# One of four transposed score tiles gets its mask from an identity product on TensorE, with a reordered start and smaller steps between

## The reference

```
inv_mask = 1.0 - attention_mask * padding_mask            # streams 0..3 only
scores = einsum('bhqd,bhkd->bhqk', q, k) / sqrt(DEPTH)
scores = scores + mask * -1e9
attn   = softmax(scores);  out = einsum('bhqk,bhkd->bhqd', attn, v)

amax    = max(abs(x2d), axis=-1)                          # int8 layer
x_scale = maximum(amax, 1e-6) / 127
x_q     = clip(round(x2d / x_scale), -128, 127)
out     = (x_q @ weight_q.T) * x_scale * weight_scale + bias
```

## Time and profile before

| | us |
|---|---|
| median of 3 runs | 1570.03 (1567.35 to 1577.67) |
| profiled execution, its own time | 1575.42 |
| its span | 1573.6 |
| PE busy | 1301.5 (83%), 5544 matmul records |
| DVE busy | 946.3 (60%) |
| ACT busy | 668.4 (42%) |
| POOL busy | 493.7 (31%) |
| granted TensorE clock, mean | 0.902 of full speed |

### The profile page before, as it was taken

One profiled execution on the slowest core, in us unless ns is written; L12 is line 12 of the kernel. 1 busy time (PEld: TensorE's weight loads), 2 busy tenths in 40 slices (PEclk: granted clock), 3 DMA queues, 4 the chain that ended last, 5 costly groups with the idle time before them and its releaser, 6 DMA issues. The chain is left out here.

```text
span 1573.6 us, 17765 instructions
## 1 busy us (share of the span) xinstructions
PE 1301.5 (83%) x5544; PEld 569.5 (36%) x5544; DVE 946.3 (60%) x2143; ACT 668.4 (42%) x1238; POOL 493.7 (31%) x676
## 2 busy tenths in 40 slices
PE   3598877878789898987997997997889856999992
PEld 1131232322324233452352352362332333556661
DVE  3699989989796665455546646647767422223334
ACT  1154545545455555535534534535546431112220
POOL 4260533522122222235335335233310103403331
PEclk9698988989899798998998997998989778999996
DMA  3833332322353532212212222223321119822225
GB/s 115 270 116 95 102 102 66 120 62 81 115 134 122 135 103 73 81 54 54 76 60 54 61 75 54 61 74 95 98 86 41 42 40 336 272 62 84 78 69 161
DMA packets 130508, 156.64 MB, mean 100 GB/s; under 512 B 15339, under 2 KB 105967, under 8 KB 130160
## 3 DMA queue, kind: packets, MB, share of 16 engines
q1 hardware_dynamic: 117872, 134.48, 28.7%
q10 hardware_dynamic: 8704, 12.58, 2.6%
q0 software_dynamic: 3840, 8.43, 1.5%
HBM read 93.92 MB, written 63.05 MB: 100 GB/s over the span
## 5 line engine op out<-in xcount | busy, mean ns | idle before, releaser
L1027 DVE TENSOR_REDUCE Mx<-bank 128x1 f32<-128x512 f32 x512 | 342.0, 686 | 304.0 <-PE bank L813 301.8
L727 ACT ACTIVATE prob<-bank 128x512 f32<-128x512 f32 x512 | 290.4, 594 | 281.0 <-PE bank L829 279.3
L813 PE MATMUL bank<-KS,QS 96*128 96x512 bf16 x768 | 319.6, 416 | 76.5 <-DVE Mx L1027 42.9
L829 PE MATMUL bank<-QS,KS 99*128 99x512 bf16 x768 | 317.2, 415 | 63.0 <-DVE prob L1038 28.4
L727 ACT ACTIVATE prob<-prob 128x512 f32<-128x512 f32 x256 | 160.9, 629 | 183.3 <-DVE prob L1038 181.5
L842 PE MATMUL bank<-prob,V 128*17 128x512 f32 x1536 | 231.3, 678 | 0.7 <-ACT prob L727 0.7
L813 PEld LDWEIGHTS bank<-KS,QS 96*128 96x128 bf16 x768 | 77.1, 100 | 302.1 <-DVE Mx L1027 115.1
L829 PEld LDWEIGHTS bank<-QS,KS 99*128 99x128 bf16 x768 | 76.8, 100 | 282.8 <-ACT prob L727 131.1
L561 POOL TENSOR_TENSOR rstd<-ve,minus_half 128x4 f32<-128x4 f32 x28 | 28.7, 1025 | 291.7 <-DVE ve L976 291.7
L581 POOL TENSOR_SCALAR MR<-neg 16x128 bf16<-16x128 f32 x48 | 13.9, 289 | 320.0 <-ACT neg L701 319.9
L1038 DVE TENSOR_TENSOR prob<-bank,ff_h 128x512 f32<-128x512 f32 x128 | 87.8, 686 | 19.1 <-PE bank L829 18.7
(11 more groups left out here) (153 smaller groups left out, 1761.8 us busy)
## 6 DMA issues: line engine op xcount, KB each, us to landing
stack_scr<-parts SPq DMA_DIRECT2D x48, 384.0 KB, 2.6
QS<-stack_scr SPq DMA_DIRECT2D x48, 384.0 KB, 4.0
KS<-stack_scr SPq DMA_DIRECT2D x48, 384.0 KB, 4.8
stack_scr<-parts SPq DMA_DIRECT2D x48, 256.0 KB, 2.9
w_gu<-in_gate_up ACTq DMA_DIRECT2D x16, 512.0 KB, 5.4
disp<-zero SPq DMA_DIRECT2D x2, 3096.0 KB, 16.1
xr<-disp SPq DMA_DIRECT2D x48, 129.0 KB, 2.1
stack_scr<-parts SPq DMA_DIRECT2D x48, 128.0 KB, 2.8
```

Of the source, the lines that this page charges most:

```text
L727: act.activation(prob[:, U % NP_, j, :], src, ACT.Exp, scale=CAST).then_inc(exp_done, 1)
L813: pe.matmul(bankS[i % NS][:, :], QS[0:STACK, v, qt * P:(qt + 1) * P], KS[0:STACK, v, :], start=True, stop=True).then_inc(s_full, 1)
L829: pe.matmul(bankT[e % NT][:, :], KS[0:ROWS, h, kt * P:(kt + 1) * P], QS[0:ROWS, h, :], start=True, stop=True).then_inc(t_full, 1)
L1027: dve.tensor_reduce(dst, b, AX.X, ALU.max).then_inc(s_read, 1)
```

## The change

Nothing is computed otherwise but for rounding. In words:

- **The product.** `PE_MASKED = 3`: in a masked stream tile j = 3 of each unit gets its mask from PE, by an f32 product of the 128x128 identity with the transposed mask (128x512), `start=True`, ahead of the score product, which now adds to it. DVE's add of that tile is gone (64 of 256), ACT exponentiates from the bank, and PE frees that bank by `exp_done` and no longer by `t_masked`.
- **The start.** The first statistics stand ahead of DVE's constants; the ones in `KS` are written by a DMA; the plain mask of sequence 0 is prepared by DVE; its transposed one by POOL, two `cut`s later than before; ACT's table is loaded by a dummy activation.
- **The int8 steps.** `xscale` is computed by POOL, the clamp is one operation of DVE, the rounding one of ACT; `i8T` is up to a step later.
- **Small steps.** `affine` and `res` go in halves; the epsilon is added by POOL's `root` and not by DVE (28 small operations less on DVE, 28 more on POOL).

```diff
+PE_MASKED = 3
...
-            put(late, s, ("turn", p, 0), ("res", p, 0))
+            put(late, s, ("turn", p, 0), *halves("res", p, 0))
...
-            put(late, s - 1, ("mask", p, 0))
+            put(late, s - 1, ("mask", p, 0), ("fill", p, 0))
             put(late, s if p == 0 else max(s, first - 6), ("mask", p, 1))
+            put(late, 5 if p == 0 else max(s, first - 6), ("fill", p, 1))
...
-                put(late, e + 20, ("amax", p), ("res", p, 4))
-                put(early, e + 21, ("quant", p))
-                put(late, e + 22, ("i8T", p))
-                put(early, e + 23, ("i8turned", p))
+                put(late, e + 20, ("amax", p), *halves("res", p, 4))
+                put(early, e + 21, ("xrec", p))
+                put(late, e + 21, ("quant", p))
+                put(early, e + 22, ("clamp", p), ("round", p))
+                put(early, e + 23, ("i8T", p))
+                put(early, e + 24, ("i8turned", p))
...
@@ SP
+                            sp.wait_ge(consts_pool, 8)
+                            sp.dma_start(KS[STACK:ROWS, :, :].rearrange("r h (c q) -> r (h c) q", q=P),
+                                         ones_b[0:ROWS - STACK, :].unsqueeze(1)
+                                         .broadcast_to([ROWS - STACK, H * S // P, P])).then_inc(ones_in, 16)
...
@@ POOL
                 def root(p, i):
                     pool.wait_ge(ve_ready[p], i + 1)
-                    link(pool.tensor_tensor(rstd[p][:, :], ve[p][:, :], minus_half[:, :], ALU.pow))
-                    link(pool.tensor_tensor(shift[p][:, :], mv[p][:, :, 0], rstd[p][:, :], ALU.mult))
-                    pool.tensor_scalar(shift[p][:, :], shift[p][:, :], -1.0, 0.0, ALU.mult, ALU.add)\
+                    pool.tensor_scalar(shift[p][:, :], mv[p][:, :, 0], -1.0, 0.0, ALU.mult, ALU.add)
+                    link(pool.tensor_scalar(rstd[p][:, :], mv[p][:, :, 1], 1e-6 if i in (1, 2, 3) else 1e-5, 0.0,
+                                            ALU.add, ALU.add))
+                    link(pool.tensor_tensor(rstd[p][:, :], rstd[p][:, :], minus_half[:, :], ALU.pow))
+                    pool.tensor_tensor(shift[p][:, :], shift[p][:, :], rstd[p][:, :], ALU.mult)\
                         .then_inc(rstd_ready[p], 1)
...
-                    link(ins)
-                    link(pool.tensor_scalar(T[p][:, :, :], T[p][:, :, :], -MAGIC, 127.0, ALU.add, ALU.min))
-                    pool.tensor_scalar(xq[p], T[p][:, :, :], -128.0, 0.0, ALU.max, ALU.add)\
-                        .then_inc(xq_ready[p], 1)
+                    ins.then_inc(grid_ready, 1)
+
+                def step_of(p):
+
+                    pool.wait_ge(amax_ready, p + 1)
+                    pool.tensor_scalar(xscale[p][:, :], amax[:, :], 1e-6, 1.0 / 127.0, ALU.max, ALU.mult)\
+                        .then_inc(xscale_ready, 1)
...
@@ ACT
-                        if n < B:
-                            act.wait_ge(t_masked, e + 1)
+                        if n < B and j != PE_MASKED:
+                            act.wait_ge(t_masked, U * (HG - 1) + j + 1)
...
+                    elif kind == "round":
+                        p = at[0]
+                        act.wait_ge(clamped, p + 1)
+                        act.activation(xq[p], T[p][:, :, :], ACT.Identity, bias=minus_magic[:, 0:1])\
+                            .then_inc(xq_ready, 1)
...
@@ PE
                     if e >= NT:
                         b = e - NT
-                        pe.wait_ge(t_masked if b < MASKED else exp_done, b + 1)
+                        if b < MASKED and b % HG != PE_MASKED:
+                            pe.wait_ge(t_masked, b // HG * (HG - 1) + b % HG + 1)
+                        else:
+                            pe.wait_ge(exp_done, b + 1)
                     h = g * HG + j
+                    on_pe = n < B and j == PE_MASKED
+                    if on_pe:
+                        if u < QT:
+                            pe.wait_ge(mask_ready[1], QT * n + u + 1)
+                        pe.matmul(bankT[e % NT][:, :], identf[:, :], mb[n % 2][:, QT + kt, :],
+                                  start=True, stop=False)
                     pe.matmul(bankT[e % NT][:, :], KS[0:ROWS, h, kt * P:(kt + 1) * P], QS[0:ROWS, h, :],
-                              start=True, stop=True).then_inc(t_full, 1)
+                              start=not on_pe, stop=True).then_inc(t_full, 1)
...
@@ DVE
-                    link(ins)
-                    dve.tensor_scalar(ve[p][:, :], mv[p][:, :, 1], 1e-6 if i in (1, 2, 3) else 1e-5, None,
-                                      ALU.add).then_inc(ve_ready[p], 1)
+                    ins.then_inc(ve_ready[p], 1)
...
-                    link(dve.tensor_scalar(xscale[p][:, :], amax[:, :], 1e-6, 1.0 / 127.0, ALU.max, ALU.mult))
...
+                def clamp(p):
+
+                    dve.wait_ge(grid_ready, p + 1)
+                    dve.tensor_scalar(T[p][:, :, :], T[p][:, :, :], MAGIC + 127.0, MAGIC - 128.0, ALU.min, ALU.max)\
+                        .then_inc(clamped, 1)
+
+                def first_mask():
+
+                    dve.wait_ge(pm_in[0], 32)
+                    link(dve.tensor_scalar(pm_row[:, :], pm_row[:, :], -1.0, None, ALU.mult))
+                    dve.wait_ge(mask_in[0][0], 16)
+                    for qt in range(QT):
+                        m = mb[0][:, qt, :]
+                        link(dve.tensor_tensor(m, m, pm_row[:, :], ALU.mult))
+                        ins = dve.tensor_scalar(m, m, 1.0, NEG, ALU.add, ALU.mult)
+                    ins.then_inc(mask_ready[0], 1)
...
-                    if n < B and 0 <= u < UNITS:
+                    if n < B and 0 <= u < UNITS and j != PE_MASKED:
                         masked(n, u, j)
```

125 lines of the change are left out of this document (75 added, 50 removed).

## The result

| | before | after |
|---|---|---|
| median, us | 1570.35 (4 runs) | 1548.98 (1542.46 to 1549.26, 4 runs) |
| profiled span, us | 1573.6 | 1547.5 |
| granted clock, mean | 0.902 | 0.920 |
| first transposed tile, us | 79.7 | 63.3 |
| masked stage (from there to stream 4's first), us | 390.5 | 393.2 |

The ratio is 0.9847, with an interval of 0.9805 to 0.989: 24 us less, and 26 by the spans. The forecast was 48 less. The direction was right and the time lies in the range, but about half of the gain isn't there. The last three rows of the table say where in these two executions: the start gave 16.5 (forecast 17), the int8 stage 12 (forecast 18), and the masks, forecast at -12, cost 3.

The account below looks back on a forecast made before the run. DVE (97% busy) was taken to bound most masked steps, PE's queue units 6 to 8, with gains hanging on the loop through PE. Masks -12, start -17, int8 -18, small steps -1: -48, from 1570.0 to 1522; range 1492 to 1560.

Parts of the forecast that it names:

- the start: From kernel start to the first transposed tile: statistics, first cut and first score come earlier; -17 us, bounds -12 and -21.
- the term of the masks, -12: All 64 masked steps: each gives DVE back 0.60 and costs PE 0.85; sum -12 us, bounds -39 and +54.
- Units 0 to 5, "0.1 to 0.2 longer", +5: Masked streams, 24 steps, nearly all with a projection: PE's loop makes each 0.1 to 0.2 us longer, +5 in all.
- the loop of 6.05: Units 0 to 5 with a projection: hand-summed loop through PE of 6.05 us, formerly 5.2, against a measured step of 5.9.
- Units 9 to 15, "I take 0.5" for 21 steps, -10: Streams 1 to 3: each step gains up to 0.55 us, taken as 0.5, over 21 steps: -10.
- The hand-closed loop of 4.27: Units 9 to 15: hand-summed loop through PE after the change, 4.27 us, where DVE's 4.84 was the longer loop before.
- Stream 0's last ten units, -9: Stream 0, units 6 to 15: -0.5 us a step by DVE and 4 us by a higher clock, together -9.
- Units 6 to 8, +2: DVE waits for PE's queue there: product's 0.85 counts whole in unit 6, perhaps a third saved next; +2 over three streams.
- The int8 term, -18: Int8 steps among the unmasked streams: DVE's 4.11 us waits and PE's idling behind them go; -18, bounds -10 and -24.
- a clamp that stands behind POOL: Int8 steps: DVE's new clamp could wait some 1.2 us behind POOL in four sequences, making the sum -43; nothing was added.
- The small steps: 28 operations of 0.17 us leave DVE, most of them where it isn't the bound: -1.
- The rival at 1552: Masks cost +10, start and int8 steps give 28: -18 in all, 1552 us; chance 0.22.

Follow-up runs that it names:

- the timed pairs: Two pairs differing in the f32 product at tile 3 alone: changed kernel without it 0.9764 against 0.9847 with it; kernel before with it alone 1590.21 us, ratio 1.008.
- the eight operations for six: Kernel before with the residual additions of stages 2 and 4 in halves, step size still on DVE: 1580.48 us, ratio 0.999.

## Why the prediction was wrong

**What failed is the term of the masks, -12; it measured +3 in the two profiled executions, and +13 by the timed pairs.** The prediction wrote off DVE in units 0 to 5 and closed the loop through PE by hand, and it put that loop too short; elsewhere it counted more steps that gain than there are. By its own steps, in the two traces:

- *Units 0 to 5, "0.1 to 0.2 longer", +5.* They were 0.46 to 0.67 longer: +12.6 over four streams. The loop was the right one, and DVE was rightly written off there; it was closed 0.30 short (product 0.96 for 0.85, 0.32 for 0.22, 0.51 for 0.42). Over a measured step of 5.9 the loop of 6.05 left 0.15; with the 0.30 it is 0.45, three times that. The product's price came from half a projection, and it holds where the product follows a score tile without a pause (0.86, 252.74 to 253.60 at tile 1). Right behind the values it is 0.96, and that is where it stands in these steps. At tile 1, where it never stands behind the values, 25 products start 0.22 after the tile ahead of them and keep PE 0.86; 37 start 0.34 or more after it and keep it 0.96.
- *Units 9 to 15, "I take 0.5" for 21 steps, -10.* They gave 6.6 over three streams, of which clock dips in streams 1 and 3 are a part. In stream 2, units 11 to 14 gained 0.45, 0.36, 0.13 and 0.95; units 9, 10 and 15, which hold turnings and a projection, gained nothing or lost up to 0.45. The hand-closed loop of 4.27 is in the trace with 4.37 to 4.39, but I counted seven plain steps where there are four.
- *Stream 0's last ten units, -9*: -5.3, at the clock that was forecast. The clock goes with the product: these units have 0.82 to 0.91 in the five traces without it, 0.97 to 1.00 in the four of the change's masked stage, and 1.00 with the product alone on the kernel before.
- *Units 6 to 8, +2*: +2.2. But the product at tile 1 wins 5.7 us a stream there, queue and clock together, so that "DVE waits for PE's queue" was read as fixed when it could be moved.

**The int8 term, -18, measured -12**: -16.5 by the edit alone, and 4.4 back by the rest of the change. What was charged to one stall was right: three times 4.1 us of DVE's, and PE's idle time behind it. Its cure was misread. The step size on POOL cures the first stall, but so do the eight operations for six, and either alone leaves the stage 8 to 11 us longer in the traces. The gain comes only with the other part of the edit, the clamp and the rounding off POOL and the turning one step later, which the prediction priced at 2 for sequence 3 and nothing for the others. That part removes the stall that stood behind the first; which half of it does so isn't shown, and by the estimate above the later turning nearly suffices. The Trainium skill ("SBUF — State Buffer", Who interferes with whom) says that the order of issue decides who blocks. The traces agree as far as they go: 4.11 us where POOL had begun 0.55 before, 0.26 where DVE was done before POOL's additions began. That DVE holds POOL up no run here shows. By the same section I had weighed a clamp that stands behind POOL; it took 0.69.

**Right**: the start (-16.5 for -17, through each of its marks) and the clock in stream 0. The small steps were put at -1; they weren't tried alone, and the halves among them moved the int8 stalls. The rival at 1552, masks that cost something while the rest gains, is what happened: chance 0.22.

## What to carry to other kernels

- Work that is moved from the bound engine to another lands in that engine's queue. Write down which long pieces then stand between two tiles that the first engine waits for, and put the new one where the queue waits anyway. Here the same product gave 37 us more at tile 1 than at tile 3.
- A loop that comes out within a few tenths of the measured step decides nothing until every gap in it is read from a row of the same neighbours. Count the steps that have the plain form before multiplying.
- A stall that is cured may have covered another, and the first cure alone then gives nothing (here the stage got 8 to 11 us longer). Ask, for the next wait on the same queue, when its partner would have been ready without the first.

## What the runs showed that was not expected

- The same f32 product keeps PE 0.86 us behind a score tile that started 0.22 us before it, and 0.96 right behind the values, or behind a tile that started 0.34 us or more before it; in bf16 it is 0.22 to 0.23. A bf16 product and a constant that bf16 holds exactly (-2^32 for -4e9) put a tile's mask on PE for a quarter of the price.
- The same one-input DVE operation of 128x4 took 0.17 to 0.26 us, or 4.11 where POOL had begun its additions first; at the start one of 0.43 took 1.37 and one of 0.69 took 1.75 beside POOL's additions.
- Two more entries in a list that is cut into quarters by its length moved an ACT operation past another. With it went 4 us of DVE in three places, without a line about either.
